# A two-layer graph network kernel on one core: 66 extra gathers in the prologue and 40 extra row loads in the first pass

## What is computed

```python
def _rgcn_layer(x, src, dst, edge_type, w_rel, root, bias):
    seg = dst * NUM_REL + edge_type
    sums = segment_sum(x[src], seg); cnt = segment_sum(ones, seg)
    mean = (sums / maximum(cnt, 1.0)[:, None]).reshape(N, NUM_REL, -1)
    return einsum('nrd,rdo->no', mean, w_rel) + x @ root + bias
edge_type = argmax(edge_attr[:, 16:26], axis=1)
h = relu(layernorm(x))
x = x + rgcn(relu(rgcn(h, w1)), w2)                  # 10 relations
h = relu(layernorm(x))
xl, xr = h @ W_l, h @ W_r                            # 4 heads of 32
score = einsum(leaky_relu(xr[dst] + xl[src]), att)
out = x + segment_softmax_sum(score, xl[src], dst) + bias
```

## Time and profile before

| | us |
|---|---|
| median of 3 runs | 15905.05 |
| the three runs | 15886.01, 15905.05, 15909.6 |
| span of the profiled execution, first to last instruction | 12719.3 |
| median of the runs less that span | 3185.8 |
| prologue, first gather of the first pass at | 666.4 |
| POOL busy, share of the span | 71% |
| DVE busy, share of the span | 42% |
| mean DMA rate over the span | 124 GB/s |

### The profile page before, as it was taken

How to read it: one execution, slowest core, us unless ns; L and a number is a source line. 1 busy time by engine, 2 the same in 40 slices (tenths; PEclk the granted TensorE clock), 3 DMA queues, 4 the chain that set the end, 5 groups by cost and what they waited for, 6 DMA issues and landing times. The chain is left out here.

```text
span 12719.3 us, 191227 instructions
## 1 busy us (share of the span) xinstructions
PE 7163.3 (56%) x34895; PEld 5987.2 (47%) x34896; DVE 5356.0 (42%) x11558; ACT 4184.5 (33%) x12473; POOL 9035.5 (71%) x9581
## 2 busy tenths in 40 slices
PE   3744444444445864444444444556777777777775
PEld 1333333333334543333333333445666666666665
DVE  7822222222222641111111111444766666666766
ACT  2522222222222222222222222224444444444442
POOL 0167777777777767777777777767777777777775
PEclk8855555555555975555555555567989999999998
DMA  8612222222222532222222222336888888888886
GB/s 244 203 51 52 53 52 52 52 53 52 52 53 71 184 119 52 53 52 52 52 53 52 52 53 53 77 93 184 237 232 231 234 233 232 234 236 231 238 235 190
DMA packets 922327, 1585.71 MB, mean 125 GB/s; under 512 B 303096, under 2 KB 487286, under 8 KB 915302
## 3 DMA queue, kind: packets, MB, share of 16 engines
q0 software_dynamic: 314112, 685.63, 21.9%
q1 hardware_dynamic: 371542, 586.31, 14.9%
q10 hardware_dynamic: 236150, 307.81, 8.3%
HBM read 1211.54 MB, written 365.75 MB: 124 GB/s over the span
## 5 line engine op out<-in xcount | busy, mean ns | idle before, releaser
L696 POOL DMA_INDIRECT p_g<-ytab,p_i x6250 | 5910.8, 946 | 1973.7 <-issue 1666.8
L662 PE MATMUL p_pg<-p_v,p_oh 128*128 x14480 | 3301.3, 411 | 4144.0 <-ACT p_v L742 4141.5
L662 PEld LDWEIGHTS p_pg<-p_v,p_oh 128*128 128x128 f32 x14480 | 2959.3, 307 | 4511.9 <-issue 4498.9
L1124 POOL DMA_INDIRECT a_g<-xlw,a_i x3125 | 2996.7, 959 | 1005.9 <-issue 886.2
L619 DVE TENSOR_TENSOR A<-p_pg,A 128x128 f32 x1448 | 421.3, 291 | 5397.9 <-PE p_pg L662 5395.5
L742 ACT ACTIVATE p_v<-p_g,wgt_all 128x128 f32<-128x128 f32 x6250 | 1960.4, 388 | 547.3 <-issue 520.4
L736 ACT ACTIVATE p_i<-rel_all 128x5 int32 (+1 forms) x1250 | 260.1, 208 | 5058.5 <-DMA p_g<-ytab,p_i 5058.5
L1534 PE MATMUL a_px<-a_g,ident 128*128 x1450 | 737.5, 594 | 853.2 <-SPq L1175 756.7
L601 DVE TENSOR_TENSOR p_oh<-p_cols,local 128x640 f32<-128x640 f32 x1456 | 1191.8, 819 | 39.6 <-DVE local L596 0.4
L1199 ACT ACTIVATE a_away<-a_dst,a_minus 128x640 f32 x727 | 602.2, 828 | 1393.9 <-issue 885.0
L1523 PE MATMUL a_pg<-a_v,a_into 128*128 128x132 f32 x7000 | 967.5, 288 | 82.7 <-issue 52.3
(11 more groups left out here) (240 smaller groups left out, 6196.9 us busy)
## 6 DMA issues: line engine op xcount, KB each, us to landing
a_xj<-xjw ACTq DMA_DIRECT2D x725, 330.0 KB
xjw<-a_g SPq DMA_DIRECT2D x625, 330.0 KB
a_dst<-in_dst_dram SPq DMA_DIRECT2D x625, 320.0 KB
p_g<-ytab,p_i POOLq DMA_INDIRECT x6250
ytab<-steps POOLq DMA_DIRECT2D x98, 640.0 KB, 3.9
ytab<-y_y SPq DMA_DIRECT2D x98, 640.0 KB
ea<-in_edge_attr_dram SPq DMA_DIRECT2D x50, 1176.0 KB
a_g<-xlw,a_i POOLq DMA_INDIRECT x3125
```

What stands on the lines that cost most here:

```text
L662: last = t.matmul(pg[k % len(pg)][:, 0:width], onehot[k][:, q * P:(q + 1) * P], V[:, ds(at + q * width, width)], start=(q == 0), stop=(q = ...
L696: pool.indirect_dma_start(gbuf[k][:, q * D:(q + 1) * D], None, rows, bass.IndirectOffsetOnAxis(ap=stage[k][:, q:q + 1], axis=0)).then_inc( ...
L1124: pool.indirect_dma_start(gbuf[k][:, q * W:(q + 1) * W], None, xlw, bass.IndirectOffsetOnAxis(ap=stage[k][:, q:q + 1], axis=0)).then_inc(s ...
```

## The change

In the prologue POOL makes a seventh constant, `probe_i`, in the last column of `A`: the numbers 1, 8, 15 and so on, one a partition. It then issues 66 indirect DMAs, six of each of eleven shapes: 128, 127, 126, 125, 124, 120, 112, 64, 32 and 16 rows of 128 numbers, and 128 rows of 384 numbers. Their rows come from the input `x` and go to columns 8000 and up of `A`. After each six it waits until all of them have landed. They count on `s_out[0]`, the semaphore of the stores, so the two waits on it become larger by 66 x 16 = 1056.

In the first pass SP reads 16 numbers of the step table into registers, loads 16 single rows of `x` at these addresses, waits, loads 8 single rows at fixed addresses, waits, loads 8 pairs of rows at register addresses, and waits. All go to the buffer `yb[0]` of the pass. Only then does it load the weights. These 32 transfers count on `s_w`, so the wait of PE becomes 560 instead of 48.

```diff
+                probe_i = A[:, NT * W - 1:NT * W].bitcast(I32)
...
-                            sp.wait_ge(s_out[k], 16 * (NT // 2))
+                            sp.wait_ge(s_out[k], 16 * (NT // 2) + (1056 if k == 0 else 0))
...
+                        nc.gpsimd.iota(probe_i, [[0, 1]], base=1, channel_multiplier=7, allow_small_or_imprecise_dtypes=True).then_inc(s_iota, 1)
+                        pool.wait_ge(s_iota, 7)
+                        seen = 0
+                        for parts, width in ((128, 1), (127, 1), (126, 1), (125, 1), (124, 1), (120, 1), (112, 1), (64, 1), (32, 1), (16, 1), (128, 3)):
+                            rows = x[0:N - 2, :].rearrange("(a k) d -> a (k d)", k=3) if width == 3 else x
+                            for n in range(6):
+                                pool.indirect_dma_start(
+                                    A[0:parts, 8000 + n * 384:8000 + n * 384 + width * D], None, rows,
+                                    bass.IndirectOffsetOnAxis(ap=probe_i[0:parts, :], axis=0)).then_inc(s_out[0], 16)
+                            seen += 96
+                            pool.wait_ge(s_out[0], seen)
...
-                                act.wait_ge(s_out[k], 16 * (i // 2))
+                                act.wait_ge(s_out[k], 16 * (i // 2) + (1056 if k == 0 else 0))
...
-                    pe.wait_ge(self.s_w, 48)
+                    pe.wait_ge(self.s_w, 560)
...
             def sync(self, sp):
+                s_probe = self.s_w
+                values = load(sp, SP_, steps, 160, 16, TOP)
+                for n in range(16):
+                    row = within(values[n], N - 1)
+                    sp.dma_start(self.yb[0][n:n + 1, 0:D], x[ds(row, 1), :]).then_inc(s_probe, 16)
+                sp.wait_ge(s_probe, 256)
+                for n in range(8):
+                    sp.dma_start(self.yb[0][n:n + 1, 0:D], x[n:n + 1, :]).then_inc(s_probe, 16)
+                sp.wait_ge(s_probe, 256 + 128)
+                for n in range(8):
+                    row = within(values[n], N - 2)
+                    sp.dma_start(self.yb[0][2 * n:2 * n + 2, 0:D], x[ds(row, 2), :]).then_inc(s_probe, 16)
+                sp.wait_ge(s_probe, 512)
```

## The result

The changed kernel took 15928.42 us in the median of 18 runs (15898.01 to 15945.46), the kernel before 15893.13 in 18 runs beside it (15862.15 to 15922.72). The ratio is 1.002, 95% interval 1.0013 to 1.0027: 35 us or 0.22% more. The forecast was 15916 us and "no change that can be told", up to 0.2%. The time lies inside the range, but the effect stands on the edge of the bound, and it is about three times the 11 us of the sum.

The account below looks back on a forecast made before the run. It took POOL's gathers to pace two passes and DVE's chain, at times held by DMA, the prologue. Terms 0 + 11 + 0 + 0 = 11 us on 15905 gave 15916 us, range 15872 to 15965.

Parts of the forecast that it names:

- the 11 us of the sum: Whole kernel: all terms together, 0 + 11 + 0 + 0 us, all from the gathers' use of the DMA engines.
- Same: Whole kernel: the main verdict, no difference above 0.2% (32 us), chance 0.80, slight lean to slower.
- The gathers on POOL: Prologue: 83 us issue plus 44 us waits, POOL done at 129 us (bounds 66 to 292), cost nothing.
- the cover of 131 us: Prologue: POOL's idle gap from its constants at 2 us to the first store at 133 us, hiding the gathers.
- The gathers on the DMA engines: Prologue: gathers push edge chunks back, 16.6 us of all sixteen engines x 0.66 = 11 us, bounds 0 and 17.
- The rule of 127 partitions: Prologue: gathers of 127 rows use one DMA engine, land 4 to 18 us later, POOL done at 133 to 147.
- First rival: Prologue: POOL finishes too late, DVE waits for ACT; 15916 up to 16032 us, chance 0.09 over the limit.
- my threshold of 176 us: Prologue, first rival: POOL must be done by 176 us or DVE is held; losing 32 us needs 208.
- Second rival: POOL's loops: moved code must be fetched anew each turn, 124 us a pass, 16040 to 16288 us, chance 0.03.
- Third rival: Outside the trace: the unseen 3185.8 us move, 15852 or 15980 us; chance 0.06 faster, 0.02 slower.
- What bounds the kernel: Passes: two paced by POOL's gathers alone, 7819 us of the span; the prologue is DVE's chain, at times held by DMA.
- Constant, waits, loads on SP: Prologue and first pass: iota 0.1 us, larger waits nothing, SP loads 21 to 85 us hidden before PE's weights; cost nothing.

Follow-up runs that it names:

- e4: Kernel before plus the 66 gathers and their eleven waits, all of 128 rows of 128 numbers, no SP loads: 15980.48 against 15967.49 us, ratio 1.0009.
- e11: Kernel before plus 66 gathers, all of 128 rows, own destinations, one wait at the end, no SP loads: 15941.08 against 15925.94 us, ratio 1.0007.
- e10: Kernel before plus only the six gathers of 127 rows with one wait: 15933.37 us, ratio 1.0002.
- e8: Kernel before plus 66 gathers of all shapes, own destinations, one wait at the end, no SP loads: 16012.15 us, ratio 1.0029.
- after: The changed kernel with gathers and SP loads, against the kernel before: median 15928.42 us, ratio 1.002; its profiled execution took 15917.56 us.
- e0: The kernel before, unchanged, profiled a second time: span 15972.6 us, time 15974.4 us.
- e6: Kernel before with POOL held ahead of its stores until VectorE's 23rd edge chunk, no transfers added: 15979.5 us, ratio 1.0007.
- e3: Kernel before plus 49 GpSimd constants of 4000 columns in the prologue, no gathers or added DMA: 16035.52 us, ratio 1.0056.
- e2: Kernel before plus the extra SP row loads only, without the gathers: 15941.89 us, ratio 0.9994.
- e5: Kernel before plus the 66 gathers, one behind each store of tiles 31 to 96, no SP loads: 16008.58 against 15925.94 us, ratio 1.0047.

## Why the prediction was right or wrong

- **Sum and value.** 11 us were forecast and 35 measured; the value is 12 us off (15916 against 15928.42, on a before that was 12 us lower in this comparison). "Same" holds only on its edge.
- **The gathers on POOL.** This is the term that went wrong. Done at 129 us was wrong, 204.8 is what came, inside the bounds of 66 to 292, and "the cost is nothing" fell with it: the cover of 131 us was used up, and the node rows cost 22.5 us more. The part that was mis-sized is the wait: ten landings took 80.6 us and the last 12.06, 8.4 us each instead of 4, which is 49 of the 76 us. The issue took 20 us more than 82.6: the 66 have 86.4 us of duration and 16.6 of ordinary issue between them. Of that the 127 rows make 10 us (2.55 for each instead of 0.94) and the two beside VectorE's long instructions 6. The pause of 6.8 us, which only runs with gathers of 127 rows show, is the rest. The worst single wait was 15.3 us, so my upper end of 18.8 was fair, and the middle should have leaned to it: six gathers issued one behind the other into busy engines land later than one gather in quiet, and that holds for even shapes as well (7.2 us each in e4).
- **The gathers on the DMA engines.** 11 us were counted, and VectorE's first statistics are 10.4 us late. The agreement is partly luck. Even shapes bring 6.5 us with waits between the groups (e4, 114.54) and 11.6 without (e11), which fits the way it was counted. For uneven shapes it fails: the six gathers of 127 rows alone, 1 us by my count (6 x 0.26 x 0.66), bring 9 (e10), and the mixed ones without waits 36 (e8).
- **The rule of 127 partitions.** I weighed it only as a later landing, POOL done at 133 to 147 us. Two effects I didn't price: such a gather keeps GpSimd 1.6 us longer, and it delays another queue's transfers, which e8 and e10 show. With even shapes POOL is free at 168.1 us (e4) instead of 204.8, on the cheap side of the first rival's threshold.
- **First rival.** Held at 0.09 for a loss over the limit, and it is what happened, in a mild form. POOL was done after my threshold of 176 us (by its own numbers 177), ACT did stand for the store of tile 0 (40.5 us in after) and VectorE did wait. The place was wrong (`stats`, for node rows, not `inverse`). The price was near: my rule that each us after 176 is lost makes 29 us at 204.8 and 17 at 193.1, and the waits for node rows are 22.5 and 12.1 us above e0's. What the rule left out is the chunks: in e6 the waits for them are 16.8 us shorter than in e0, in after they are not.
- **Second rival.** Gone: queues of instructions carry 205 and 320 packets in after against 204 and 319 in before (205 and 319 in e0).
- **Third rival.** The records of after and e0 leave no fifth unseen; the first profile was of another execution, and the pauses that make the difference are in both kernels.
- **What bounds the kernel.** "Two passes paced by POOL alone" was true of the 12719.3 us execution only. In after the 6250 gathers take 5896.9 us and the pauses before them 3872.3, of which 1933.0 wait for ACT. A delay in the prologue still comes through to the end, since the passes begin only after it: in e3 the reciprocals are 82 us later than in e0 and the median is 81 us longer.
- **Constant, waits, loads on SP.** As forecast: nothing (e2: 0.9994). The forecast's 1 us for a register load, and so 16 of its 85 us, is in no run by itself; loads of registers, rows and waits together lie inside the 51 us.

What stays open: why ACT, VectorE and TensorE stand together for up to 27 us in the passes of all executions but the first profiled one, on which engines the rows of an uneven gather go, and what POOL stands for before the sixth gather of 125 rows. How much of the 35 us is uneven shapes and how much the lateness that they and the waits cause is bounded only: all of one shape costs 0.0 to 0.18% (e4), no lateness but uneven 0.17 to 0.41% (e8), lateness alone up to 0.16% (e6). Kernels without gathers in front and with a first store by 193 us came to their reciprocals between 642.5 and 659.0 us, and the same prologue with gathers at 674.5 and 701.4. So single differences of under 17 us there are not to be read, and larger ones not to the us.

## What to carry to other kernels

Before costing an insertion into an idle stretch, compare the profiled span with the timed runs: if a fifth is missing, the profile may show another execution, and its bottleneck may not be the one timed. Price an added DMA twice, by what its issuer waits for and by what it does to the transfers of other queues; prefer 128 partitions to 127, since six gathers of 127 rows were seen to delay the first statistics of another engine by 9 us and to keep GpSimd 1.6 us longer each. Compare an oddly long instruction with another shape at the same moment before blaming its shape: what looked like a price of 126 rows was a neighbour's long instruction. And to test "this engine is late" use a wait on something that comes later anyway, not busy work on the engine, which may hold its neighbour.

## What the hardware did that I had not expected

- An indirect DMA of 127 rows keeps GpSimd for 2.55 us, of 128 rows 0.94, of 126 rows 0.97 when nothing holds it; 128 rows of 384 numbers cost 0.95 to 1.41, hardly more than of 128 numbers.
- Beside long instructions of VectorE a gather of 128 rows takes 3.4 to 4.1 us (e4, e11), and beside its scans of 6.9 us one took 7.54 (e5). That VectorE holds it is read from the times alone.
- In the other direction, GpSimd's constants of 4000 columns stretched a tensor_scalar of VectorE from 170 to 3327 ns.
- A register-addressed load of two rows takes SP 3.87 us to issue (8 in 30.98 us), where 16 of one row took 8.02 us, 0.50 each.
- The same kernel ran in 12719 us once under the profiler and between 15.86 and 16.00 ms in all its timed executions.
